# A decoder layer with routed experts: GpSimd's part of the norms and the routing, batch 3's mixing, PSUM homes, placement order and weight fills rearranged

## The chip, the cores and the metric

One core of a Trainium2 chip runs the kernel in one launch. The metric is device time in microseconds (us), the median over the runs shown. Engines are TensorE (PE; PEld its weight loads), VectorE (DVE), ScalarE (ACT), GpSimd (POOL) and SyncE (SP, which only issues DMAs here).

## What is computed

x is [4, 256, 256], the context [4, 256, 64]. Each of three sublayers is added to x:

```python
x = x + attn(layernorm(x))                 # 16 heads of 16, rotary positions, causal softmax, Wout
x = x + xattn(ctx, layernorm(x))           # per batch: (1 - g) * n + g * (A + A.T) / 2, g = sigmoid(gamma_raw), n = layernorm(x)
x = x + ffn(layernorm(x))                  # 64 experts, 6 per token, plus one shared expert
```

In xattn, sim is a 256 x 256 similarity of context rows, A keeps sigmoid(sim) where sim is among the 76 largest of its row. In ffn, the router's sigmoid scores plus a bias are looked at in 8 groups of 8; a group's score is the sum of its two largest; the 4 best groups stay, and of their experts the 6 best are taken. An expert has room for 48 tokens; the outputs are weighted by the scores (normalised, times 2.5) and summed.

## The kernel before

The 1024 tokens are 8 tiles of 128 (partitions), two tiles to a batch. The first stage does attention, mixing and routing batch by batch; then all chosen token rows lie in a DRAM table `slot_rows` (one row per expert slot), and the second stage goes over the experts in pairs: it gathers a group's slots, transposes, multiplies, and scatters the results to `expert_rows`; a tail adds them up per token and writes the output.

**The order is written by hand.** `STEPS` (L61) is one list of steps. Every engine walks it in order and executes its own part of each step; a number behind a step is the batch. The steps the text speaks of:

- A1 to A2: norm 1, projections, rotary positions, split in three bfloat16 parts. `U0` to `U5`: six score units. In step U of batch b, TensorE makes a T unit of batch b-1 and an S unit of batch b; ScalarE takes the exponentials of the T unit (L805), VectorE the row maxima of the S unit (L1168). In batch "4" only T units are left. `MS`/`MT`: the maxima split in parts (L1180 to L1183), and turned by TensorE (L513, copied at L1157). `ME`: the last PV product.
- D1a: the adjacency turned (L541) and added to itself (L1187). D1b, D1c, D1d: head outputs turned (L549), averaged (L1192, L1195), turned again (L557). D1e: output projection (`project_out`, L566), VectorE's residual (L1200) with norm 2's statistics (L1088, L1095), GpSimd's inverse root (`inverse_root`, L891 to L902).
- D2: mixing. ScalarE scales the adjacency with the norm's shift (L760), VectorE adds it to the scaled residual (L1209) and takes norm 3's statistics; GpSimd makes that root.
- D3a: ScalarE writes x3, the normed rows (L744), TensorE turns them (L574), ScalarE copies (L823). D3b: router (L584) and sigmoid (L829).
- `F n`: n steps of VectorE's adjacency work (MAX8 and MATCH_REPLACE, L1057, L1062). `R n` selects routing group n, `G n` runs n steps of VectorE's routing (L1224 to L1320; the last writes the places). `P n`: TensorE counts positions of group n (L613), between routing's selection (L1284) and the scan that is the last reader of that PSUM area (L1310). Groups 0 to 3 are the batches.
- `Z n`: GpSimd stores n slot rows (`place_rows`, L996). Each is an indirect DMA of one of a tile's six choices; 12 belong to a group, 48 in all. Those of group n wait for `place_ready` n + 1. The last group's 12 stand behind the list, behind three memsets (L1011 to L1013).

PSUM has four areas: `unit` (two halves in turn), `proj`, `gen` and `out`. `AREAS` and `USES` list from STEPS who uses an area in which order; a writer waits until the previous user has freed it.

SP's queue holds the input loads, the q/k stacks, the zeroing of the two DRAM tables, and the expert weights of pairs 0 to 21 (`later`, L359): one pair at A2d1, one at A2d2, 11 at D3a1 (which waits for the last T unit of batch 2 and all adjacency rows), 9 at D3a3. Behind them stand the waits for all placements, and the gathers.

Of the kernel before, what the change touches and what calls it, by code (L numbers as in the profile page):

```python
# [11 lines left out]
ALU = mybir.AluOpType  # L12
ACT = mybir.ActivationFunctionType
# [51 lines left out]
    D1d0 U12 A2d3 D1e0 U22 F5 U32 D20 U42 F1 D1a2 U52 F1 MS2 V0 F1 ME2 MT3 D1b1 F5 D1c1 D3a0 F6 D3b0 G9 U03 D1d1 G7 U13  # L65
    F1 D1e1 G7 U23 G4 U33 D21 U43 Z2 F1 G5 Z1 G2 P0 U53 MS3 G5 D3a1 ME3 MT4 D1b2 F4 D3b1 Z3 D1c2 R1 G1 U04 F3 G13 Z1 D1d2
    F1 Z3 U14 G2 U24 F3 D1e2 Z3 G16 U34 G5 F5 P1 U44 D22 U54 ME4 D1b3 G5 D1a3 Z1 D3a2 F1 D1c3 Z5 G5 D1d3 F2 Z4 F1 G2 D1e3
    F1 Z2 F1 D3b2 G1 R2 Z1 G48 F1 D23 Z1 P2 Z5 D3a3 F1 D3b3 Z4 F1 R3 MS4 G1
# [8 lines left out]
        "P": ("gen", "pos")}  # L77
NORMS = []
for _st, _b in STEPS:
    if _st in USES:  # L80
        AREAS[USES[_st][0]].append((USES[_st][1], _b))
# [9 lines left out]
AREAS["proj"] += [("sd", 1)]  # L91

# [4 lines left out]
def decoder_kernel(nc, x, cosT, sinT, ctxT, wxT, wqkvT, woT, gamma, gate_w, bias, w_gu, w_dn, ws_gu, ws_dn, out):  # L97
# [3 lines left out]
    with ExitStack() as ctx:  # L101
# [109 lines left out]
        gpen = cut(MO, NT, NG)  # L211
# [61 lines left out]
        var_ready, norm_ready, spread_ready = sem("var_ready"), sem("norm_ready"), sem("spread_ready")  # L273
        xn_ready, shuffled, sin_done, roped, part0, rest_ready, part1, part2 = (
# [41 lines left out]

        def probs_at(key):
            return prob[:, T_UNITS.index(key), :]
# [9 lines left out]
        def _(sp):  # L328
# [30 lines left out]
            later = {("A2d", 1): range(0, 1), ("A2d", 2): range(1, RA - 6), ("D3a", 1): range(RA - 6, RA + 5), ("D3a", 3): range(RA + 5, RP)}  # L359
            for stage, b in STEPS:  # L360
# [11 lines left out]
                if (stage, b) == ("D3a", 1):  # L372
                    filled(sp, "unit", (T_UNITS[-1], 2))
                    sp.wait_ge(adj_row, B)
                if (stage, b) == ("D3a", B - 1):
                    filled(sp, "gen", ("att", B - 1))
                for p in later.get((stage, b), ()):
                    ring_fill(p)
# [27 lines left out]
        def _(pe):  # L406
# [129 lines left out]
            def adjacency_turned(b):  # L536
                claim("gen", ("aT", b))
                pe.wait_ge(adj_row, b + 1)
                for i in range(TPB):
                    for j in range(TPB):  # L540
                        last = nc.tensor.transpose(gen[:, i * S + j * P:i * S + (j + 1) * P], adj[:, TPB * b + j, i * P:(i + 1) * P], identf[:, :])  # L541
                last.then_inc(full["gen"], 1)
# [17 lines left out]
            def project_out(b):  # L560
                claim("gen", ("att", b))
                emptied(pe, "gen", ("onT", b))
                pe.wait_ge(wo_in, 16)
                for t in range(TPB):
# [922 lines left out]
```

## Time and profile before

| what | us |
|---|---|
| median of 3 runs | 293.35 (292.18 to 296.54) |
| span of the profiled execution | 299.4 |
| busy: TensorE / VectorE / ScalarE / GpSimd | 226.2 / 207.2 / 95.6 / 134.1 |
| first slot row issued, last one issued | 133.43, 209.28 |
| first expert transpose | 217.95 |

The profile is of one execution; its span runs from its first to its last instruction, and is 6.05 us longer than the runs' median. "Idle before, releaser" names what ended an engine's idle time; "issue" and "remote" stand where no instruction of the profile explains it. The strips cut the span in 40 slices of 7.5 us.

### The profile page before, as it was taken

The numbers are of one execution on the slowest core, as the hardware profiler recorded it, in microseconds if no ns is written. First come the engines' busy times: TensorE is split into PE (matmuls) and PEld (weight loads), VectorE is DVE, ScalarE is ACT, GpSimd is POOL, SyncE is SP. The second block draws the span as 40 slices with busy tenths as digits, with TensorE's granted clock in tenths as the row PEclk, the third lists the DMA queues.
The fourth block names the chain that finished last, engine by engine and source line by source line (L and its number), as shares of the span: only waits on it lengthen the run. The fifth ranks groups of instructions, "written<-read, shape, count | busy, mean of one in ns | idle before, by whom it ended". The sixth has DMA issues, their size and how long they took to land.

```text
span 299.4 us, 5226 instructions
## 1 busy us (share of the span) xinstructions
PE 226.2 (76%) x1836; PEld 165.8 (55%) x1836; DVE 207.2 (69%) x668; ACT 95.6 (32%) x154; POOL 134.1 (45%) x182
## 2 busy tenths in 40 slices
PE   8883586598889888879566214494989999896993
PEld 3672475486678577659335103243457766653882
DVE  3699999979989998987692671912145334751697
ACT  1444530522434555566154014010013333333000
POOL 2810767616115300236677757777204655673000
PEclk9999589599999999999978755588699999999899
DMA  6608979694085999923208999990599999921996
GB/s 213 195 0 108 106 110 168 95 124 87 0 107 78 305 398 382 350 72 134 93 27 259 283 283 298 300 244 14 107 200 211 255 262 217 279 83 41 378 387 198
DMA packets 36890, 55.78 MB, mean 186 GB/s; under 512 B 6556, under 2 KB 26790, under 8 KB 36864
## 3 DMA queue, kind: packets, MB, share of 16 engines
q1 hardware_dynamic: 31680, 47.75, 62.6%
q10 hardware_dynamic: 768, 3.54, 5.7%
q0 software_dynamic: 4416, 4.15, 4.8%
q8 instruction: 15, 0.25, 0.4%
q14 instruction: 11, 0.09, 0.1%
HBM read 32.93 MB, written 25.17 MB: 194 GB/s over the span
## 4 chain that ended last, share of the span: by engine, by line
POOL 18%; PE 15%; issue 11%; DVE 10%; DMA 6%; another core or an unknown queue 4%; ACT 2%; ACTq 0%; POOLq 0%; SPq 0%; DVEq 0%
POOL slot_rows L996 15%; PE unit L644 5%; PE proj L663 3%; DMA arena<-expert_rows 2%; DVE arena L1432 2%; DMA arena<-slot_rows 2%; PE unit L630 2%; DVE arena L1168 2%; PE outp L653 1%; DVE arena L1434 1%; POOL rstd L897 1%; DVE arena L1438 1%; DMA slot_rows<-rows,arena 1%; DVE arena L1436 1%
## 5 line engine op out<-in xcount | busy, mean ns | idle before, releaser
L996 POOL DMA_INDIRECT slot_rows<-rows,arena x48 | 47.6, 992 | 23.9 <-issue 12.1
L1018 POOL DMA_INDIRECT expert_rows<-arena x28 | 28.3, 1010 | 34.0 <-ACT arena L870 27.5
L805 ACT ACTIVATE arena<-unit 128x1024 f32<-128x1024 f32 x24 | 24.6, 1024 | 42.8 <-PE unit L488 37.4
L1168 DVE TENSOR_REDUCE arena<-unit 128x4 f32<-128x1024 f32 (+1 forms) x24 | 28.9, 1212 | 3.1 <-PE unit L475 3.1
L1057 DVE MAX8 arena<-arena 128x8 f32<-128x256 f32 x80 | 30.6, 414 | 0.3
L488 PE MATMUL unit<-arena 128*128 128x256 bf16 (+1 forms) x128 | 29.2, 248 | 0.0
L1062 DVE MATCH_REPLACE8 arena<-arena 128x256 f32<-128x256 f32 x72 | 29.0, 409 | 0.0
L487 PE MATMUL unit<-arena,identb 128*128 128x128 bf16 x128 | 25.8, 222 | 0.0
L895 POOL TENSOR_SCALAR nmean<-mv 128x2 f32<-128x2 f32 x12 | 2.8, 236 | 46.0 <-DVE mv L1095 41.4
L486 PE MATMUL unit<-arena 96*128 96x128 bf16 (+1 forms) x96 | 22.3, 253 | 0.6 <-ACT arena L805 0.6
L475 PE MATMUL unit<-arena,identb 128*128 128x128 bf16 x128 | 20.8, 227 | 0.0
L855 ACT ACTIVATE arena<-unit 128x192 f32<-128x192 f32 (+1 forms) x18 | 5.6, 314 | 43.2 <-PE unit L644 27.4
L1411 DVE TENSOR_TENSOR arena<-arena,unit 128x192 f32<-128x192 f32 (+1 forms) x18 | 5.9, 330 | 19.3 <-ACT arena L855 16.7
L474 PE MATMUL unit<-arena 96*128 96x128 bf16 (+1 forms) x96 | 16.5, 257 | 3.3 <-DVE arena L1168 3.2
L456 PE MATMUL proj<-arena 128*128 128x256 f32 x64 | 16.6, 417 | 1.3 <-ACT arena L768 1.3
L870 ACT ACTIVATE arena<-proj,arena 128x256 f32<-128x256 f32 x32 | 13.6, 471 | 11.2 <-PE proj L663 6.4
L499 PE MATMUL outp<-arena 128*32 128x256 f32 x128 | 11.6, 404 | 5.5 <-ACT arena L792 4.7
L456 PEld LDWEIGHTS proj<-arena 128*128 128x128 f32 x64 | 13.3, 213 | 3.5 <-ACT arena L768 1.5
L1402 DVE COPY arena<-unit 128x384 f32<-128x384 f32 (+1 forms) x18 | 9.0, 507 | 8.4 <-PE unit L630 8.2
L487 PEld LDWEIGHTS unit<-arena,identb 128*128 128x128 bf16 x128 | 12.8, 100 | 1.2
L488 PEld LDWEIGHTS unit<-arena 128*128 128x128 bf16 x128 | 12.8, 100 | 1.1
L475 PEld LDWEIGHTS unit<-arena,identb 128*128 128x128 bf16 x128 | 13.1, 102 | 0.2
(221 smaller groups left out, 550.9 us busy)
## 6 DMA issues: line engine op xcount, KB each, us to landing
ring<-in_w_gu SPq DMA_DIRECT2D x16, 384.0 KB
expert_rows<-blank SPq DMA_DIRECT2D x8, 768.0 KB, 9.5
arena<-in_w_gu SPq DMA_DIRECT2D x16, 384.0 KB, 13.3
arena<-expert_rows SPq DMA_DIRECT2D x7, 768.0 KB, 9.2
slot_rows<-blank SPq DMA_DIRECT2D x1, 4608.0 KB, 17.3
arena<-slot_rows ACTq DMA_DIRECT2D x12, 288.0 KB
arena<-ring_dn SPq DMA_DIRECT2D x24, 128.0 KB, 4.5
ring_dn<-in_w_dn SPq DMA_DIRECT2D x16, 192.0 KB
```

The costliest lines, as they stand in the source:

```text
L456: last = mm(proj[:, m * S:(m + 1) * S], wqkv[:, c, m * P:(m + 1) * P], xnT[:, b % 2, c, :], start=(c == 0), stop=(c == 1))
L474: mm(area, qst[b % 3][0:KT, h, t * P:(t + 1) * P], kst[b % 3][0:KT, h, 0:n], start=True, stop=False)
L475: last = mm(area[:, n - P:n], identb[:, :], masks, start=False, stop=True)
L486: mm(area, kst[b % 3][0:KT, h, kt * P:(kt + 1) * P], qst[b % 3][0:KT, h, kt * P:S], start=True, stop=False)
L487: mm(area[:, 0:P], identb[:, :], masksT, start=False, stop=False)
L488: last = mm(area, sel[:, h:h + 1].broadcast_to((P, P)), nmT[:, kt * P:S], start=False, stop=True)
L805: act_fn(prob[:, n, :], unit_at((key, b)), ACT.Exp, scale=D ** -0.5).then_inc(unit_free((key, b)), 1)
L996: pool.indirect_dma_start(out=slot_dram, out_offset=bass.IndirectOffsetOnAxis(ap=place[:, t, k:k + 1], axis=0), in_=rows[:, t, :], in_offs ...
L1018: pool.indirect_dma_start(out=z_dram, out_offset=bass.IndirectOffsetOnAxis(ap=rowi[:, p:p + 1], axis=0), in_=yrow[:, p % NY, :], in_offset ...
L1057: last[i] = mark(v.max(best[:, i, :], simS[:, t + i, :] if r == 0 else work[:, i, :]))
L1062: last[i] = mark(v.match_replace(work[:, i, :], best[:, i, :], simS[:, t + i, :] if r == 0 else work[:, i, :], NEG))
L1168: v.tensor_reduce(nmax[:, t, c * u:c * u + c], unit_at((key, b)).rearrange("p (h k) -> p h k", k=n), axis=AX, op=ALU.max, negate=True).the ...
```

## The change

1. **GpSimd's roots.** For norms 2 and 3 of batches 2 and 3 (`LATE` = 2) VectorE adds eps to the variance (`variance_shifted`), GpSimd makes only the power, and VectorE the rest (`inverse_root` of VectorE).
2. **Pair sums.** For groups 0 and 1 the group score is the largest of the sums of two of its eight scores. A new step `H` on GpSimd writes the biased scores twice in a row and four sets of pair sums; VectorE takes one maximum over 32 of them in place of eleven small steps. Groups 2 and 3 keep the old way. All groups: the penalty and its addition become one instruction per tile.
3. **Batch 3.** The mixing needs no shift from ScalarE: ScalarE only scales the adjacency, VectorE scales, shifts and adds; VectorE writes x3 too. The residual goes in two halves.
4. **PSUM homes.** att of batch 3 in `proj`; the turned adjacency of batch 3 and positions 1 and 2 in `unit`; router logits of batches 2 and 3 in `out`.
5. **Order.** x3 of ScalarE has a step of its own (`N`). Of the places of F, G, Z, P and D steps many are new. Routing groups 0 and 1 have 26 steps, the others 37.
6. **Fills.** Pairs 8 to 10 are fetched at U5 of batch 2, 2 to 7 at U5 of batch 3, 11, 12 and 14 to 21 at D1b3, 13 at D1e3.

```diff
-    D1d0 U12 A2d3 D1e0 U22 F5 U32 D20 U42 F1 D1a2 U52 F1 MS2 V0 F1 ME2 MT3 D1b1 F5 D1c1 D3a0 F6 D3b0 G9 U03 D1d1 G7 U13
-    F1 D1e1 G7 U23 G4 U33 D21 U43 Z2 F1 G5 Z1 G2 P0 U53 MS3 G5 D3a1 ME3 MT4 D1b2 F4 D3b1 Z3 D1c2 R1 G1 U04 F3 G13 Z1 D1d2
-    F1 Z3 U14 G2 U24 F3 D1e2 Z3 G16 U34 G5 F5 P1 U44 D22 U54 ME4 D1b3 G5 D1a3 Z1 D3a2 F1 D1c3 Z5 G5 D1d3 F2 Z4 F1 G2 D1e3
-    F1 Z2 F1 D3b2 G1 R2 Z1 G48 F1 D23 Z1 P2 Z5 D3a3 F1 D3b3 Z4 F1 R3 MS4 G1
+    D1d0 U12 A2d3 D1e0 U22 F5 U32 D20 U42 F1 D1a2 U52 F1 MS2 V0 F1 ME2 MT3 D1b1 F5 D1c1 N0 D3a0 F6 D3b0 H0 F4 U03 D1d1 F3 U13
+    F1 D1e1 F3 U23 G6 U33 D21 U43 G8 F1 U53 MS3 P0 G12 N1 D3a1 ME3 MT4 D1b2 F4 D3b1 Z2 H1 Z1 D1c2 F2 U04 F5 D1d2 F2 U14 F2
+    U24 F3 D1e2 Z2 R1 G14 U34 D22 Z4 F2 U44 G4 F2 U54 P1 ME4 N2 G4 Z3 D1b3 D3a2 F2 D1c3 D1a3 G4 D1d3 D3b2 R2 D1e3 Z4 G4 D23 Z4 G6 N3 G15 P2
+    D3a3 G4 D3b3 G8 Z4 R3 MS4
...
+BESIDE = (("D3b", B - 2), ("D3b", B - 1))
+UNIT = (("D1a", B - 1), ("P", 1), ("P", 2))
+LATE = B - 2
...
+                if (stage, b) == ("U5", 2):
+                    filled(sp, "unit", (T_UNITS[-1], 1))
+                    fills(RA, RA + 1, RA + 2)
+                if (stage, b) == ("U5", 3):
                     filled(sp, "unit", (T_UNITS[-1], 2))
+                    fills(*range(RA - 6, RA))
+                if (stage, b) == ("D1b", 3):
+                    filled(sp, "out", (1, 3))
                     sp.wait_ge(adj_row, B)
+                    fills(RA + 3, RA + 4, *range(RA + 6, RP))
+                if (stage, b) == ("D1e", 3):
+                    filled(sp, "proj", ("att", B - 1))
+                    fills(RA + 5)
...
+                if kind != "ln1" and b >= LATE:
+                    late = n - NORMS.index(("ln2", LATE))
+                    gp.wait_ge(var_late, late + 1)
+                    gp.wait_ge({"ln2": spread_ready, "ln3": x3_ready}[kind], b)
+                    pool.tensor_tensor(rstd[:, k, :], srs[:, :], cexp[:, 0:1].broadcast_to((P, TPB)), ALU.pow).then_inc(root_ready, 1)
+                    return
...
+            def group_sums(n):
+
+                ts = slice(TPB * n, TPB * n + TPB)
+                emptied(gp, *LOGITS[n])
+                if n >= 1:
+                    gp.wait_ge(place_ready, n)
...
+                pool.tensor_tensor(twice[:, :, :, 0:8], g8, b8, ALU.add)
+                link(pool.tensor_tensor(twice[:, :, :, 8:12], g8[:, :, :, 0:4], b8[:, :, :, 0:4], ALU.add))
+                for k in range(4):
+                    end = pool.tensor_tensor(pairs[:, :, :, k, :], twice[:, :, :, 0:8], twice[:, :, :, k + 1:k + 9], ALU.add)
+                end.then_inc(group_ready, 1)
...
             place_rows(NT * KE - TPB * KE - (NT * KE - len(placements)))
-            gp.wait_ge(x3_ready, B)
-            filled(gp, "gen", ("att", B - 1))
+            gp.wait_ge(x3_last, 1)
+            filled(gp, "proj", ("att", B - 1))
...
+            def inverse_root(kind, b):
+
+                n = NORMS.index((kind, b)) - NORMS.index(("ln2", LATE))
+                k = int(kind[2]) - 1
+                ve.wait_ge(root_ready, n + 1)
...
+                if kind == "ln2":
+                    need(mark(v.tensor_scalar(rstd[:, k, :], rstd[:, k, :], gam[:, 2:3], None, ALU.mult)))
+                    mark(v.tensor_scalar(grow[:, :], rstd[:, k, :], 1.0, None, ALU.add))
+                v.scalar_tensor_tensor(shift[:, k, :], mv[:, k, :, 0], -1.0, rstd[:, k, :], ALU.mult, ALU.mult).then_inc(norm_late, 1)
+                normed(ve, kind, b)
...
+                    ends = []
+                    for t in range(TPB):
+                        r = res[:, TPB * b + t, :]
+                        ends.append(mark(v.tensor_scalar(r, r, grow[:, t:t + 1], shift[:, 1, t:t + 1], ALU.mult, ALU.add)))
+                    for t in range(TPB):
+                        r = res[:, TPB * b + t, :]
+                        ve.wait_ge(mix_scaled, t + 1)
+                        need(ends[t])
+                        end = mark(v.tensor_tensor(r, r, mix[:, t, :], ALU.add))
...
+                if n < LATE:
+                    ve.wait_ge(group_ready, n + 1)
+                    biased = twice[:, :, :, 0:8]
+                    done = mark(v.tensor_reduce(gsum[:, ts, 0:NG], pairs.rearrange("p t g k j -> p t g (k j)"), axis=AX, op=ALU.max))
+                    yield
...
+                for t in range(nt):
+                    done = mark(v.scalar_tensor_tensor(cand[:, t0 + t, 0:NE].rearrange("p (g j) -> p g j", g=NG),
+                                                       gout[:, t0 + t, 0:NG].unsqueeze(2).broadcast_to((P, NG, NE // NG)), -NEG / 10,
+                                                       biased[:, t], ALU.subtract, ALU.min))
+                    yield
```

## Rows read from the trace of the kernel before

**Rows 1.** The page: span and strips of 40 slices

```profile
span 299.4 us, 5226 instructions
...
POOL 2810767616115300236677757777204655673000
PEclk9999589599999999999978755588699999999899
DMA  6608979694085999923208999990599999921996
```

**Rows 2.** The chain of waits: start, us, what

```profile
195.23 0.97 POOL slot_rows L996
...
209.28 2.83 DMA slot_rows<-rows,arena
212.22 5.59 DMA arena<-slot_rows
217.95 0.63 PE unit L630 x4
```

**Rows 3.** GpSimd's timeline: start, us, instruction, idle before and releaser

```profile
133.43 1.24 POOL L996 DMA_INDIRECT slot_rows<-rows,arena  x1 [4.65 <-DVE arena L1320]
...
169.62 0.97 POOL L996 DMA_INDIRECT slot_rows<-rows,arena  x1 [0.30 <-issue]
170.66 0.23 POOL L895 TENSOR_SCALAR nmean<-mv 128x2 f32<-128x2 f32 x1
...
171.25 0.72 POOL L897 TENSOR_TENSOR rstd<-srs,cexp 128x2 f32<-128x2 f32 x1
...
193.72 0.99 POOL L1011 MEMSET arena<- 128x1024 f32 x1
```

**Rows 4.** Groups of instructions by form: count, busy, mean ns, idle before

```profile
L996 POOL DMA_INDIRECT slot_rows<-rows,arena x48 | 47.6, 992 | 23.9 <-issue 12.1 <-DVE arena L1320 6.9 <-POOL shift L901 2.0
...
L949 POOL TENSOR_TENSOR arena<-arena 128x1024 f32<-128x1024 f32 x3 | 7.1, 2354 | 7.7 <-DVE arena L1125 7.6
...
L901 POOL TENSOR_TENSOR shift<-nmean,rstd 128x2 f32<-128x2 f32 x12 | 2.5, 205 | 1.0
```

**Rows 5.** Timelines of VectorE, ScalarE and TensorE, 118 to 166 us

```profile
118.63 0.69 DVE L1200 TENSOR_TENSOR res<-res,gen 128x512 f32<-128x512 f32 x1 [0.22 <-PE gen L566]
...
129.56 0.42 DVE L1310 TENSOR_TENSOR_SCAN arena<-keep,arena 128x128 f32<-128x128 f32 x1
...
132.35 0.17 DVE L1320 TENSOR_SCALAR arena<-arena 128x16 int32<-128x16 f32 x1
...
144.41 0.69 DVE L1200 TENSOR_TENSOR res<-res,gen 128x512 f32<-128x512 f32 x1 [3.55 <-remote]
...
165.78 0.69 DVE L1200 TENSOR_TENSOR res<-res,gen 128x512 f32<-128x512 f32 x1 [5.17 <-issue]
...
137.17 1.03 ACT L805 ACTIVATE arena<-unit 128x1024 f32<-128x1024 f32 x1
...
151.27 1.09 ACT L760 ACTIVATE arena<-adj,shift,gam 128x256 f32<-128x256 f32 x2 [0.15 <-POOL shift L901]
153.36 1.02 ACT L805 ACTIVATE arena<-unit 128x1024 f32<-128x1024 f32 x1 [1.00 <-PE unit L488]
...
148.27 0.22 PE L613 MATMUL gen<-arena,tri 128*128 128x128 bf16 x1 [2.01 <-issue]
...
162.48 3.27 PE L566 MATMUL gen<-arena 128*128 128x256 f32 x8 [0.72 <-ACT arena L818]
```

**Rows 6.** VectorE's timeline: routing of groups 1 and 3

```profile
148.20 0.29 DVE L1289 TENSOR_TENSOR arena<-arena 128x128 f32<-128x128 f32 x1
...
150.75 0.17 DVE L1320 TENSOR_SCALAR arena<-arena 128x16 int32<-128x16 f32 x1
...
186.01 0.29 DVE L1224 TENSOR_TENSOR arena<-arena,biasb 128x128 f32<-128x128 f32 x1 [7.76 <-issue]
...
193.89 0.85 DVE L1320 TENSOR_SCALAR arena<-arena 128x16 int32<-128x16 f32 x1
```

More of the change, by code:

```diff
@@ L91 @@
 AREAS["proj"] += [("sd", 1)]
+LOGITS = [("out" if ("D3b", n) in BESIDE else "gen", ("lg", n)) for n in range(B)]
 def nth(area, name):
@@ L357, in stack, with fills @@
                             sp.dma_start(to, src).then_inc(stack_in[b], 16)
-            later = {("A2d", 1): range(0, 1), ("A2d", 2): range(1, RA - 6), ("D3a", 1): range(RA - 6, RA + 5), ("D3a", 3): range(RA + 5, RP)}
+            def fills(*pairs):
+                for p in pairs:
+                    ring_fill(p)
             for stage, b in STEPS:
@@ L536, in adjacency_turned @@
             def adjacency_turned(b):
-                claim("gen", ("aT", b))
+                area, to = ("unit", unit_at(("aT", b))) if b == B - 1 else ("gen", gen)
+                claim(area, ("aT", b))
                 pe.wait_ge(adj_row, b + 1)
@@ L583, in router @@
                         g = TPB * b + t
-                        last = mm(gen[:, t * NE:(t + 1) * NE], x3T[:, c, g * P:(g + 1) * P], gatew[:, c, :], start=(c == 0), stop=(c == 1))
-                last.then_inc(full["gen"], 1)
+                        last = mm(to[:, t * NE:(t + 1) * NE], x3T[:, c, g * P:(g + 1) * P], gatew[:, c, :], start=(c == 0), stop=(c == 1))
+                last.then_inc(full[area], 1)
             def shared_in(n):
@@ L820, in x3_dims @@
             def x3_dims(b):
-                moe_input(b)
                 filled(sc, "gen", ("x3T", b))
@@ L1240, in routing @@
                     need(lo)
[L1241 removed]
+                    done = mark(v.tensor_tensor(gsum[:, ts, 0:NG], tg(hi3), tg(lo3), ALU.add))
                     yield
[L1243 to L1248 removed]
@@ L1249, in routing @@
-                done = mark(v.tensor_tensor(gsum[:, ts, 0:NG], tg(hi3), tg(lo3), ALU.add))
-                yield
+                    biased = sbias[:, ts].rearrange("p t (g j) -> p t g j", g=NG)
                 need(done)
@@ L1309, in routing @@
                 yield
-                v.tensor_tensor_scan(fl(rank[:, ts]), fl(keep[:, 0:nt, :]), fl(kept[:, ts]), 0.0, ALU.mult, ALU.add).then_inc(free["gen"], 1)
+                v.tensor_tensor_scan(fl(rank[:, ts]), fl(keep[:, 0:nt, :]), fl(kept[:, ts]), 0.0, ALU.mult, ALU.add).then_inc(read, 1)
                 yield
```

220 lines of the change are left out of this document (152 added, 68 removed).

## The prediction

> **What bounds the kernel now.** I read the page's share rows first, then the chain of waits, then GpSimd's timeline, then VectorE's, and last ScalarE and TensorE where the first stage ends. No engine is busy throughout; but GpSimd's strip, broken by low slices elsewhere, stays at five or more in the ten slices from 135 to 210 us [rows 1]. The chain says why that stretch decides: from 195.23 to 210.25 us it is nothing but slot rows (a row is one indirect store of 128 tokens, issued by GpSimd); the last starts at 209.28, its data lands at 212.1, the gather reads take until 217.8, and the first expert transpose starts at 217.95 [rows 2]. The 89.2 us behind 210.25 are not touched by the change. So what it is worth is how far it moves the end of the 48th row.
>
> A row takes 0.99 us in the mean and follows its neighbour at 1.28 (0.97 busy, 0.31 issue) [rows 3, 4]. Forty-eight rows are 61.4 us of the 76.8 between 133.43 and 210.25. Between them lie four inverse roots of layer norms (2.2 to 3.3 us each with the gaps around them; the third one, 170.59 to 173.46, is shown in part) and three memsets (1.4 us) [rows 3]. The last twelve rows wait for two things: GpSimd must be through the other 36 and the memsets, at 195.06, and VectorE must have written the last group's places, at 194.74 [rows 3, 6]. The two feeders are 0.3 us apart. The kernel gains only if both come earlier, and loses if either comes later.
>
> **The queue order, counted.** GpSimd executes in program order, so a row listed behind a root waits for that root's input. Counted in the step list (Z steps), rows ahead of each root are: before, 10 ahead of norm 2 of batch 2, 13 ahead of norm 3 of batch 2, 23 ahead of norm 2 of batch 3, 26 ahead of norm 3 of batch 3; the timeline has the 23rd at 169.62, straight ahead of the third root [rows 3]. After: 3, 5, 12 and 16. I call the moment at which the power of norm 2, batch 3, can run **A**. Behind A there were 25 rows; now there are 36.
>
> Behind A the changed queue holds: the power, 0.75 with a gap of 0.5 behind it [rows 3]; 4 rows, 5.1; the second power with its gap, 1.25; 8 + 12 rows, 25.6; the memsets, 1.5; the last 12 rows, 11 x 1.28 + 0.97 = 15.05. Sum 49.75. Before, the first power of this pair started at 171.25 and the end came 39.0 later. The last row ends at A + 49.75, so A must be at 160.5 for no change at all. That is 5.3 us before the residual that feeds it starts in the present trace (165.78) [rows 5]. The question is therefore how early A comes.
>
> **What GpSimd sheds and takes on.** Each of the four late roots keeps only the power (0.75); the negated mean, the eps, the gamma factor, the growth and the shift (0.2 to 0.5 each [rows 4]) go to VectorE. A full root runs from 170.66 to 172.97, 2.3 us, so about 1.5 us x 2 for norm 2 and 0.9 x 2 for norm 3, 4.8 in all, is saved. The pair sums of batches 0 and 1 add six small tensor_tensor each. No such shape is in the trace: bounds are 0.2 us (the 128x2 one) and 2.35 us (128x1024) [rows 4]; 128 elements by the slope between them are about 0.47, so 2.8 us a call, 1.2 to 14 by the bounds. Batch 0's lies in GpSimd's idle time before 120 and costs nothing; if it took 14 us VectorE would wait for it at 122. Batch 1's stands between rows 2 and 3 of the new order, ahead of a point where GpSimd waits anyway.
>
> The Trainium skill speaks against moving elementwise sums there: GPSIMD Engine Reference, Engine selection, has additions on VectorE, GpSimd being about twice as slow for two inputs. VectorE does 128x128 in 0.29 us, so by that rule a sum would be about 0.6; the call is 3.5 then and the forecast does not move.
>
> **VectorE up to the first places.** Up to the residual at 118.63 nothing changes. From there the new order is: residual and statistics 1.6 [rows 5]; three adjacency steps 1.1; reduction 1.14; six routing steps (max over the pair sums, taken as 0.7: between 0.29 for 128 and 1.21 for 1024 elements [rows 4, 5]; then two MAX8, a copy, two replacements 0.9) 1.6; reduction 1.14; mixing with statistics 1.8; reduction 1.14; eight routing steps 1.9 (from the penalty to the selection); one adjacency step 0.4; sum 11.8, to 130.4. Then the last reduction 1.14 and the shift parts 0.85, to 132.4. The twelve steps that were spread before all come behind these: 2.2 us to the end of the scan and 2.7 to the places, as the same lines take from 148.20 [rows 6]. So the places of group 0 are written at 135.2 against 132.52, and the PSUM home "gen" is freed by that scan at 134.6 against 129.98 [rows 5]. The x3 transposes of batch 1 claim gen next; they followed at 131.4 and now start at 134.7. TensorE works in order: behind them stand the last PV of batch 2, MT4, D1b2, the router and the first T unit of batch 3. That unit's exponential, at 137.17 before [rows 5], comes about 3.1 later. What the edits save on VectorE (11 small routing steps of 0.17 to 0.3 per group, 2.3 us, against 0.7 for the max) is spent on ten adjacency steps brought forward, so it doesn't cover this.
>
> **From there to A.** The residual of batch 2 ran at 144.41, after a pause of 3.55 us that no instruction explains [rows 5]. If the pause does not recur, three microseconds later means 144.4 again; if it does, 147.5. Then on VectorE: residual and statistics 1.8, fourteen routing steps 3.5 (1.6 + 1.9) that now stand ahead of the root's remainder, the three small operations 0.7; ScalarE's scaling of the adjacency 1.15 [rows 5]; mixing 0.87, statistics 0.95, eps 0.2. The variance of norm 3 of batch 2 is ready at 144.4 + 9.2 = 153.6, up to 156.7. GpSimd has then placed 5 rows and stands idle, where it had placed 13. Its power with gap (1.25) and seven rows (8.95) take it to 163.8 to 166.9. That is one lower bound for A.
>
> The other is the attention of batch 3. ScalarE runs the scaling of batch 2 ahead of the exponentials of U4 and U5, so these cannot start before the mixing input is out, 151.6 to 154.7, and end two microseconds later, 153.6 to 156.7 (before: 154.38). From there to the residual the trace has 11.4 us [rows 5], and 1.8 to the variance. The new order takes 1.0 off (the transposed adjacency no longer stands ahead of the head average) and 0.5 by halves. A = 165.3 to 168.4; if TensorE keeps its upper clock (2.4 GHz) for project_out, about 1.8 instead of 3.27 us [rows 5], 163.8. The wait for positions of group 1 that held TensorE before 148.27 is gone, 2.0 us [rows 5], but it lay where ScalarE now waits for the scaling instead.
>
> Both bounds meet; I take A = 166.0, between 163.8 and 168.4. The last row ends at 215.75 against 210.25, +5.5 (ends +3.3 and +7.9).
>
> **The other feeder.** From A: the halves and mixing on VectorE leave norm 3 ready before GpSimd's power, at A + 1.25 + 5.1 + 0.75 = 173.1; x3 0.9, fifteen routing steps 3.7, positions 1.0, x3T 1.1, copy 0.6, router 1.9, sigmoid 0.3: 182.6 against 186.0. With 8.73 us of routing as before (186.01 to 194.74) [rows 6] the last places are written at 191.3, 3.4 earlier than now. GpSimd reaches the last twelve at 200.7. The change shortens the chain it aims at, and the rows that it moves behind the chain cost more. The other homes (gen, out, unit) serve this feeder, and cost nothing while it has 9 us to spare. The weight fills start at about 123 and 130 instead of 156.78, into a stretch where the DMA strip is at 3 or less; rows don't suffer, since they kept 1.28 us in the slices of full DMA load too, 165 to 202 [rows 1, 3]. I price them at 0.
>
> VectorE's new small operations may also be held by GpSimd: one L1320 took 0.85 beside the memset against 0.17 for the others [rows 6]. Eight such operations are new on the way from A to x3; 0 to 0.68 each is 0 to 5.4 us. I take 0, as for 3 of the 4 rows; the slack of 9 us covers the far end, the part ahead of A (two of them) would cost up to 1.4. The Trainium skill has this rule (SBUF — State Buffer, Who interferes with whom): VectorE and GpSimd share one pair of ports under an exclusive lock, and tensor_scalar and copies in the two-port mode are held for a whole GpSimd instruction. This trace agrees in that one row.
>
> **Forecast.** The profiled execution spans 299.4; the runs' median is 293.35, 6.05 less, and I carry that difference over. 299.4 + 5.5 - 6.05 = 298.85.
>
> **Rivals.**
> - *The rows don't bind (faster).* If the waits from 137 to 150 were the old order's own and the last exponential ends by 145, A falls at 157 and the last row ends at 206.75, 3.5 earlier: 289.85. For it: the unexplained pause of 3.55 us before the residual of batch 2, and TensorE's wait of 2.01 behind P1, which goes [rows 5]. Against it: the gen home freed 4.6 later, and the scaling behind fourteen routing steps. It decides from A = 160.5 on, one us per us. Chance 0.14; only A below 154.6 is over 2%, which can be told from no change.
> - *It washes out.* Pauses fall elsewhere, A near 160.5: 293.35. Chance 0.2.
> - *The chain is late as well.* Pause kept, half clock in project_out, held VectorE operations: A = 170.5, last row at 220.25, +10: 303.35. For it: TensorE's granted clock, in tenths, falls to 5 (1.2 of 2.4 GHz) in the three slices from 172.5 to 195, where TensorE is idle for long stretches, and project_out took 3.27 us at 162.48 [rows 1, 5]. Chance 0.16.
> - *The change doesn't do what it says*: GpSimd's pair sums cost 14 us and VectorE waits at 122: over 303, inside the last chance.
>
> **Numbers.** Forecast 0.5, own range 296 to 302. Of it a little under half lies above 299.2, where slower by over 2% begins (2% is about what a measurement of this kernel can tell from no change; the lower bound is 287.5). Slower 0.16 + 0.24 = 0.40; faster 0.08, part of the first rival, and rounded up to 0.1; same 0.50. For 8 in 10 the range runs from 288.5 to 304.
>
> **What would show it.** Right: places of group 0 at about 135; 5 rows done before the power of norm 3, batch 2, with two idle stretches of GpSimd over 3 us between 138 and 155; the residual of batch 3 at 164 to 166; the last places near 191 and the last row near 216; no idle of GpSimd from about 167 on. Wrong: the last twelve rows starting within 1 us of the last places (the feeder of VectorE binds), or A before 160.

## The result, and the profile after

The changed kernel took 304.04 us (302.7 and 305.37) against 292.86 of the kernel before beside it (292.18 to 296.54): ratio 1.0375, 95% interval 1.0257 to 1.0493. Medians here and below leave out runs over 1.5% above the fastest of their kernel in the same set, a slower state that any kernel can fall in (here 308.65 and 309.16, with which the median is the 307 of some recorded expectations). The kernel is slower. The forecast of 298.85 had the direction of the shift and was 5.2 us too low; 304.04 lies at the upper edge of the wide range (304) and above the narrow one (302). The largest single chance, 0.50, stood on no change clear of noise; slower, which came, had 0.40.

The page of the kernel after, the strips that answer to [rows 1]:

```profile
span 301.0 us, 5221 instructions
...
POOL 2811677615205312306336687787701566674000
```

In the two slices from 142.5 to 157.5 us GpSimd's strip reads 3 and 3 where it had 6 and 7, and the one from 210 us reads 7 where it had 2: work has moved from the first place to the second. GpSimd's timeline of the kernel after shows it exactly (start, us, instruction, idle before and its releaser), and answers to [rows 3]:

```profile
134.99 1.24 POOL L1077 DMA_INDIRECT slot_rows<-rows,arena  x1 [6.99 <-DVE arena L1481]
...
139.94 0.46 POOL L1057 TENSOR_TENSOR arena<-arena,biasb 128x128 f32<-128x128 f32 x1 [2.43 <-ACT arena L890]
140.36 0.32 POOL L1058 TENSOR_TENSOR arena<-arena,biasb 128x64 f32<-128x64 f32 x1
140.76 1.51 POOL L1060 TENSOR_TENSOR arena<-arena 128x128 f32<-128x128 f32 x4
...
147.47 0.72 POOL L957 TENSOR_TENSOR rstd<-srs,cexp 128x2 f32<-128x2 f32 x1 [4.05 <-DVE srs L1287]
...
154.48 0.71 POOL L957 TENSOR_TENSOR rstd<-srs,cexp 128x2 f32<-128x2 f32 x1 [3.78 <-DVE srs L1287]
...
167.26 0.71 POOL L957 TENSOR_TENSOR rstd<-srs,cexp 128x2 f32<-128x2 f32 x1 [3.06 <-DVE srs L1287]
...
173.47 0.73 POOL L957 TENSOR_TENSOR rstd<-srs,cexp 128x2 f32<-128x2 f32 x1
...
199.82 0.98 POOL L1092 MEMSET arena<- 128x1024 f32 x1
...
215.42 0.98 POOL L1077 DMA_INDIRECT slot_rows<-rows,arena  x1 [0.30 <-issue]
```

Ahead of the first three late roots GpSimd stands idle for 3 to 4 us, and from A (167.26) on it never does. The 36 rows behind A, with the two powers and the memsets, fill the time to 216.40. This is the picture that the forecast drew. Lines of VectorE, ScalarE and TensorE in the kernel after, answering to [rows 5] and [rows 6]:

```profile
133.92 0.17 DVE L1481 TENSOR_SCALAR arena<-arena 128x16 int32<-128x16 f32 x1
...
145.48 0.69 DVE L1307 TENSOR_TENSOR res<-res,gen 128x512 f32<-128x512 f32 x1 [2.54 <-PE gen L614]
...
165.07 0.42 DVE L1319 TENSOR_TENSOR res<-res,proj 128x256 f32<-128x256 f32 x1 [1.28 <-PE proj L614]
...
190.12 0.16 DVE L1481 TENSOR_SCALAR arena<-arena 128x16 int32<-128x16 f32 x1
...
141.17 1.03 ACT L866 ACTIVATE arena<-unit 128x1024 f32<-128x1024 f32 x1
...
163.87 1.97 PE L614 MATMUL proj<-arena 128*128 128x256 f32 x8
```

The residual of batch 2 has no "remote" pause in front of it here; before it had one of 3.55 us [rows 5]. The last places (190.12) are 11 us ahead of the last twelve rows (201.31). They no longer bind. The first expert transpose of the kernel after:

```profile
223.95 0.63 PE L682 MATMUL unit<-identf,arena 128*128 128x128 f32 x4 [1.29 <-DMA arena<-slot_rows]
```

| us | before | after | |
|---|---|---|---|
| end of the last slot row | 210.25 | 216.40 | +6.15 |
| from there to the first expert transpose | 7.70 | 7.55 | -0.15 |
| from there to the end of the span | 81.45 | 77.05 | -4.40 |
| span | 299.4 | 301.0 | +1.6 |
| median of the runs (293.35, 304.04), less the span | -6.05 | +3.04 | +9.09 |

So within the profiled executions the first stage lost about what was forecast (+6.15, forecast +5.5), and the second stage, which the change does not touch, was 4.4 us shorter. The last row is the riddle: the profile of before is an execution longer than its runs, that of after (302.7) the shortest of its own.

### The profile page after: what moved, and what is told of

Same layout as the page of the kernel before. It is cut to its first block, busy times and chain, and to the rows that moved or that the text cites. A ratio compares the mean times of both kernels' runs of the same rounds, so it can differ in the third digit from the quotient of the medians.

```text
span 301.0 us, 5221 instructions
## 1 busy us (share of the span) xinstructions
PE 222.9 (74%) x1836; PEld 165.5 (55%) x1836; DVE 207.6 (69%) x663; ACT 94.8 (31%) x152; POOL 134.9 (45%) x178
## 3 DMA queue, kind: packets, MB, share of 16 engines
q10 hardware_dynamic: 768, 3.54, 5.8%
## 4 chain that ended last, share of the span: by engine, by line
PE 21%; POOL 15%; DVE 12%; issue 10%; DMA 6%; ACT 2%; POOLq 0%; SPq 0%; ACTq 0%; DVEq 0%
POOL slot_rows L1077 13%; PE unit L696 7%; PE proj L715 4%; PE unit L682 2%; DMA arena<-expert_rows 2%; DVE arena L1593 2%; DMA arena<-slot_rows 2%; DVE arena L1249 2%; PE outp L705 2%; DVE arena L1595 1%; DVE arena L1599 1%; PE proj L596 1%; DMA slot_rows<-rows,arena 1%; PE outp L545 1%; POOL rstd L957 1%
## 5 line engine op out<-in xcount | busy, mean ns | idle before, releaser
L532 PE MATMUL unit<-arena 96*128 96x128 bf16 (+1 forms) x96 | 21.7, 247 | 0.6 <-ACT arena L866 0.6
L520 PE MATMUL unit<-arena 96*128 96x128 bf16 (+1 forms) x96 | 16.4, 256 | 2.8 <-DVE arena L1249 2.8
L671 PE MATMUL outp<-ones 128*128 128x384 bf16 x30 | 7.6, 432 | 13.9 <-DMA slot_rows<-rows,arena 13.9
L962 POOL TENSOR_SCALAR nmean<-mv 128x2 f32<-128x2 f32 x8 | 1.8, 227 | 35.4 <-DVE mv L1176 30.9
L671 PEld LDWEIGHTS outp<-ones 128*128 128x128 bf16 x30 | 3.7, 125 | 17.9 <-issue 17.1
L533 PEld LDWEIGHTS unit<-arena,identb 128*128 128x128 bf16 x128 | 12.6, 98 | 1.1
```

The costliest lines, as they stand in the source:

```text
L532: mm(area, kst[b % 3][0:KT, h, kt * P:(kt + 1) * P], qst[b % 3][0:KT, h, kt * P:S], start=True, stop=False)
L533: mm(area[:, 0:P], identb[:, :], masksT, start=False, stop=False)
```

## The experiments

Kernels with the same median of the kernel before in the table ran on one chip, beside it. The chips differ, so only such kernels, or ratios to the kernel before, are compared. GpSimd's queue and the second stage in each profile:

| kernel | before beside it, median | ratio, 95% interval | rows ahead of the four roots | A | end of last row | second stage |
|---|---|---|---|---|---|---|
| before | | | 10, 13, 23, 26 | 171.25 | 210.25 | 81.45 |
| before again | 301.00 | 1.0007 (0.9917 to 1.0096) | same | 170.78 | 210.24 | 81.4 |
| before, rows held back | 293.97 | 1.0282 (1.0141 to 1.0424) | 3, 5, 12, 16 | 164.11 | 217.40 | 77.15 |
| before, early fills | 301.73 | 1.0007 (0.9967 to 1.0048) | 10, 13, 23, 26 | 171.73 | 209.61 | 83.7 |
| after | 292.86 | 1.0375 (1.0257 to 1.0493) | 3, 5, 12, 16 | 167.26 | 216.40 | 77.05 |
| after again | 293.97 | 1.0424 (1.0285 to 1.0563) | same | 167.48 | 216.71 | 77.3 |
| after, old fills | 293.97 | 1.0315 (1.0184 to 1.0447) | same | 167.07 | 216.20 | 77.2 |
| after, order of before | 293.97 | 1.0172 (1.0039 to 1.0305) | 10, 13, 23, 26 | 169.99 | 211.00 | 76.9 |
| rows spread | 301.00 | 1.0324 (1.0204 to 1.0444) | 6, 11, 15, 19 | 173.04 | 218.72 | 81.8 |
| positions 0 in `unit` | 301.00 | 1.0354 (1.0261 to 1.0446) | 3, 5, 12, 16 | 169.93 | 220.86 | 82.7 |
| group 1 forward | 301.00 | 1.0497 (1.0405 to 1.0589) | 6, 11, 20, 24 | 177.77 | 223.47 | 81.5 |
| new order | 301.73 | 1.0104 (1.0062 to 1.0145) | 7, 11, 19, 25 | 168.69 | 212.24 | 83.5 |
| new order, old fills | 301.73 | 1.0011 (0.9964 to 1.0057) | 7, 11, 19, 25 | 164.13 | 211.11 | 81.3 |
| new order, mended | 299.64 | 1.0062 (1.0017 to 1.0106) | 7, 11, 20, 24 | 165.60 | 209.53 | 81.3 |

**The kernel before again**, with no edit.

> The kernel before, unchanged, for a second profile. The profiled execution on record spans 299.4 us where the runs' median is 292.9, and it holds pauses that no instruction explains (3.55 us ahead of the residual of batch 2, 3.7 and 4.1 us in the expert stage). Theory (queue order explains the 14 us): a typical execution lacks most of these pauses, spans about 291, and its last row ends at 205 to 208 instead of 210.25, so that the changed kernel's 216.4 is 8 to 11 us later and not 6. Rival (the second stage pays too): the last row ends at 210 again, the span is still 291 to 293, and the changed kernel must lose the rest behind its last row.

Measured: 300.95 us (300.65 to 303.64) where the same kernel had had 293.35. VectorE's timeline of this execution:

```profile
143.83 0.69 DVE L1200 TENSOR_TENSOR res<-res,gen 128x512 f32<-128x512 f32 x1 [3.54 <-remote]
...
165.49 0.69 DVE L1200 TENSOR_TENSOR res<-res,gen 128x512 f32<-128x512 f32 x1 [5.46 <-issue]
```

The pause of 3.55 us in front of the first residual is there again (3.54), and so is the long second stage. The profiled run took 300.65 us with a span of 298.8. The profile of before, with 299.4, therefore shows an execution of about 301, such as this chip gives, beside runs whose median was 293.35; whether it came from another chip than those runs is not on record. Neither expectation held: the last row ended at 210.24 again, as the rival had it, but the span was not 291 to 293.

**Rows held back, in the kernel before.** Nothing but GpSimd's queue is changed.

```diff
-    ... D3b1 Z3 D1c2 R1 G1 U04 F3 G13 Z1 D1d2
-    F1 Z3 U14 G2 U24 F3 D1e2 Z3 G16 ... D1c3 Z5 G5 ...
-    ... R2 Z1 G48 ...
+    ... D3b1 D1c2 R1 G1 U04 F3 G13 D1d2
+    F1 U14 G2 U24 F3 D1e2 Z2 G16 ... D1c3 Z2 G5 ...
+    ... R2 Z2 G48 ...
```

> The kernel before with nothing changed but the rows: 3, 5, 12 and 16 of them ahead of the four late roots, as in the changed kernel. Theory (queue order): the third root comes at 169 to 171 as before or up to 2 us earlier, eleven more rows stand behind it at 1.28 us, 14.1 us; the last row ends 11 to 14 us later than in the kernel before, ratio 1.036 to 1.048. Rival (rows are not what binds, the end is set by VectorE's places or by pauses): ratio 0.99 to 1.01.

Measured: 302.48 us (301.24 to 303.39) against 293.97, 8.5 more; the ratio of 1.028 is below the 1.036 that was expected, and the last row ended 7.15 us later, not 11 to 14. GpSimd's third root and VectorE's two residuals in it:

```profile
164.11 0.72 POOL L897 TENSOR_TENSOR rstd<-srs,cexp 128x2 f32<-128x2 f32 x1
...
141.42 0.69 DVE L1200 TENSOR_TENSOR res<-res,gen 128x512 f32<-128x512 f32 x1 [0.51 <-PE gen L566]
...
161.74 0.69 DVE L1200 TENSOR_TENSOR res<-res,gen 128x512 f32<-128x512 f32 x1 [5.41 <-PE gen L566]
```

Behind A stand 53.3 us against 39.0, 14.3 more: the eleven rows at 1.28 (14.1), as counted. A is 7.14 earlier, which I had not expected, and its parts can be read. The residual of batch 3 comes 4.04 earlier, 2.99 of it because the pause in front of the residual of batch 2 is missing (141.42 against 144.41 [rows 5]). And the power follows that residual by 2.37 instead of 5.47 us: in the kernel before the root waits 3.1 us behind a row [rows 3]. The other 1.05 us of the earlier residual is not traced. Net of the pause, the held-back rows put the end of the last row about 10 us later (14.3 - 3.1 - 1.05). The queue order alone, with nothing else of the change, made the kernel 2.8% slower.

**The changed kernel again**, with no edit.

> The changed kernel again, as the measure for the variants that run beside it. If the whole loss is the kernel's own, the ratio to the kernel before is 1.03 to 1.045 here too. If the first measurement was wide by chance and my queue count (+5.5 us) is right, it is 1.012 to 1.025. The last slot row should start near 215.4 us and the power of norm 2 of batch 3 (A) near 167.

Measured: 305.44 us (302.6 to 306.08), 11.5 above the kernel before, where the first measurement had 11.2; the loss is the kernel's own, and 216.71 and 167.48 are where they were expected.

**The changed kernel in the order of the kernel before.** The whole step list of before, with N0, H0, H1, N1, N2, N3 put in and eleven G steps taken from each of groups 0 and 1; for instance:

```diff
-    ... U24 F3 D1e2 Z2 R1 G14 U34 D22 Z4 F2 U44 G4 F2 U54 P1 ME4 N2 G4 Z3 D1b3 ...
+    ... U24 F3 D1e2 Z3 G16 U34 G5 F5 P1 U44 D22 U54 ME4 D1b3 G5 D1a3 Z1 N2 D3a2 ...
```

> The changed kernel with every cheaper operation and every new PSUM home kept, but with the step list of the kernel before (slot rows 10, 13, 23 and 26 ahead of the four late roots; routing of group 0 and its places where they were; x3 of each batch on its engine straight ahead of its transposes). Theory (the queue order costs the time): A falls at 164 to 169 and behind it stand 25 rows instead of 36, power and gap 1.25, 3 rows 3.8, power 1.25, 10 rows 12.8, memsets 1.5, last twelve 15.05, in all 35.7 us, so the last row ends at 200 to 205 if the last places are there by 190, and no later than 210 if they bind; the ratio to the kernel before is 0.965 to 1.00 and GpSimd has no idle stretch over 3 us between 150 and 165. Rival (the loss lies in the operations themselves, in pauses of TensorE, or behind the slot rows): the last row ends at 212 or later and the ratio stays at 1.025 or more.

Measured: 298.50 us (296.33 to 299.59). It lies between the two expectations: 6.9 us of the 11.5 come back with the order, but there is no gain on the kernel before. TensorE and GpSimd show why:

```profile
148.21 0.27 PE L665 MATMUL unit<-arena,tri 128*128 128x128 bf16 x1 [4.71 <-issue]
...
164.41 3.75 PE L614 MATMUL proj<-arena 128*128 128x256 f32 x8 [0.72 <-issue]
...
177.70 0.98 POOL L1077 DMA_INDIRECT slot_rows<-rows,arena  x1 [5.77 <-DVE arena L1481]
```

TensorE waits 4.71 us for group 1's selection (written at 148.10) ahead of the last two T units, and project_out took 3.75 us (granted clock 0.50) where it took 1.97 (1.00) in the changed kernel. A came at 169.99, straight behind the 23rd row, so the rows ahead of it held it as well. What GpSimd saves on its roots it loses waiting for group 2's places.

**The fills.** Two pairs: the changed kernel with the old fills, and the kernel before with the new ones.

```diff
-                if (stage, b) == ("U5", 2):
-                    filled(sp, "unit", (T_UNITS[-1], 1))
-                    fills(RA, RA + 1, RA + 2)
...
+                if (stage, b) == ("D3a", 1):
+                    filled(sp, "unit", (T_UNITS[-1], 2))
+                    sp.wait_ge(adj_row, B)
```

> The changed kernel with the weight fills back at their old places in SyncE's queue (all of them behind the last adjacency rows, the last four behind the attention of batch 3). Theory (fills cost nothing in either place): within 1% of the changed kernel run beside it, the last row starts within 1 us of its 215.4. Rival (the early fills disturb TensorE or VectorE through memory or DMA traffic): 1 to 3% faster than the changed kernel, fewer pauses of TensorE between 120 and 165.

> The kernel before with nothing changed but the weight fills, which go as early as in the changed kernel. Theory (early fills cost in part of the executions): ratio 1.005 to 1.012. Rival, and what my prediction priced (0): ratio 0.995 to 1.004, the last row within 0.5 us of 210.25.

Measured: 302.78 us (302.46 to 303.69) with old fills beside 305.44 with early ones, though the profiled executions of the two are as good as one (spans 300.7 and 300.8). In the kernel before early fills changed nothing (1.0007, twelve runs; the last row ended at 209.61), as the rival had it. Alone the first pair proves little, with four runs each; the next experiment has the same pair again.

**A new order**, meant to be faster than both: the old order up to group 0's places, the last T units straight behind each other, positions of group 1 behind them, fewer rows ahead of the first late root. The lines taken out are those of the changed kernel in the order of the kernel before.

```diff
-    F1 Z3 U14 G2 U24 F3 D1e2 Z3 G16 U34 G5 F5 P1 U44 D22 U54 ME4 D1b3 G5 D1a3 Z1 N2 D3a2 F1 D1c3 Z5 G5 D1d3 F2 Z4 F1 G2 D1e3
+    F1 U14 G2 U24 F3 D1e2 Z4 G9 U34 U44 U54 P1 D22 Z1 ME4 G14 N2 D1b3 D1c3 Z7 D1d3 D3a2 F11 D1e3
-    F1 Z2 F1 D3b2 G1 R2 Z1 G48 F1 D23 Z1 P2 Z5 N3 ...
+    D3b2 D1a3 R2 Z6 G48 F1 D23 Z1 P2 Z5 N3 ...
```

> The changed kernel's parts in a new order: routing of group 0 and its places as in the kernel before; the last two softmax units of batch 3 straight behind the third, the positions of group 1 behind them; norm 2 of batch 2 with 7 rows ahead instead of 10; batch 3's head average ahead of the last adjacency steps; routing of group 2 in one piece behind the residual of batch 3. Theory (GpSimd's queue and VectorE's order together set the end, so both must be right): the last exponentials end near 149 instead of 155 us, A comes at 163 to 166 with 19 rows ahead, behind it stand 29 rows, 37.1 us, two powers with gap and the memsets, 4.0 us; the last row ends at 204 to 208 against 210.25 before, 211.0 in the order of the kernel before and 216.7 in the changed kernel; ratio to the kernel before 0.975 to 0.995. Rival (the attention chain of batch 3 is held by something else, so that A stays at 168 to 170): the last row ends at 209 to 213 and the ratio is 1.00 to 1.02.

> The same order with the weight fills at their old places in SyncE's queue. With the changed kernel's own order the old places gave a median 3 us lower, though both profiled executions had the same length. Theory (early fills cost some us in part of the executions, through pauses that come and go): 2 to 3 us below the same order with early fills. Rival (chance between executions): within 1 us of it.

Measured: 305.12 us with early fills and 302.02 with old ones, twelve runs each on one chip; ratios 1.0104 and 1.0011, and their intervals do not touch. Early fills cost 0.9% in this order. The two profiles around the last T units, by stretches of 5 us (length, then busy time with number of instructions for PE, PEld, DVE, ACT and POOL, granted clock, share of the DMA engines, GB/s); with early fills:

```profile
140.00:145.00 5.00, 5.00 (x61) 4.15 (x60) 3.36 (x17) 1.65 (x2) 4.18 (x7) 1.00 1.03 362
145.00:150.00 5.00, 3.73 (x37) 2.16 (x34) 4.28 (x23) 1.94 (x2) 3.48 (x5) 1.00 1.05 354
```

and with old ones:

```profile
140.00:145.00 5.00, 5.00 (x65) 3.62 (x64) 4.77 (x20) 1.28 (x2) 3.93 (x5) 1.00 0.32 115
145.00:150.00 5.00, 2.52 (x38) 1.67 (x35) 2.87 (x19) 3.27 (x5) 3.47 (x5) 1.00 0.24 86
```

The DMA engines are full in one and a quarter to a third full in the other, and the fourth exponential of batch 3 runs at 147.48 against 143.87. Of these 3.6 us 1.45 were there at 95 us already, long before the first of the early fills; about 2.2 arise here. That the full DMA load is what delays it is suggested by this one pair of profiles and not shown, and no run shows how.

With early fills all three figures fell as the rival had them: A at 168.69, the last row's end at 212.24, the ratio at 1.0104. With old fills A came as expected (164.13, expected 163 to 166), but the last row did not (211.11). GpSimd in that kernel:

```profile
176.52 0.98 POOL L1067 DMA_INDIRECT slot_rows<-rows,arena  x1 [5.31 <-DVE arena L1471]
```

My order had group 2's router and the turned adjacency behind project_out, so that group's places were late (176.07).

**That fault mended**: the router ahead of project_out, the turned adjacency added behind group 2's routing, old fills.

```diff
-    ... N2 D1b3 D1c3 Z7 D1d3 D3a2 F11 D1e3
-    D3b2 D1a3 R2 Z6 G48 F1 D23 Z1 P2 Z5 N3 ...
+    ... N2 D1b3 D3a2 D1c3 Z8 D1d3 D3b2 F11 D1e3
+    R2 Z4 G48 D1a3 D23 Z3 P2 Z5 N3 ...
```

> The new order with old fills, with one fault mended: there GpSimd stood idle for 5.31 us until the places of group 2 at 176.07, because VectorE's routing of that group waited for TensorE to run project_out, the router and the transposes of the last adjacency in this order. Now the x3 transposes of batch 2 and the router come ahead of project_out, and the transposed adjacency is added behind the routing. Theory (with the places in time GpSimd has no idle stretch left): A at 164 to 167.5 (TensorE's router costs up to 1.3 us of it) with 20 rows ahead, places of group 2 at 171 to 174, last row ends at 204.5 to 208, ratio to the kernel before 0.975 to 0.993. Rival (TensorE's pauses and held VectorE steps take the gain, wherever the steps stand): places of group 2 at 175 or later, last row at 209 or later, ratio 0.996 to 1.01.

Measured: 301.86 us (299.18 to 303.22), ratio 1.0062, last row ended at 209.53. A (165.60) and the places of group 2 (172.75) came as expected, the end did not, for a reason of my own making:

```profile
172.75 0.17 DVE L1471 TENSOR_SCALAR arena<-arena 128x16 int32<-128x16 f32 x1
...
176.72 0.71 POOL L947 TENSOR_TENSOR rstd<-srs,cexp 128x2 f32<-128x2 f32 x1 [5.33 <-DVE srs L1277]
```

I had listed only 24 rows ahead of the fourth root, so GpSimd waited for that root with group 2's rows ready from 172.9. Three rows fitted there, 3.8 us. The rival (other pauses eat the gain) is neither shown nor refuted; no version here is faster than the kernel before.

**Three edits of the changed kernel** that loosen one link each: more rows ahead of the roots (Z4 behind H1, Z5 at D1e2, Z1 at D22, none at N2, Z3 more ahead of D1e3's root); positions 0 in `unit`, so that `gen` is free earlier; and group 1's routing and its rows brought forward.

```diff
-... D3b1 Z2 H1 Z1 D1c2 ... D1e2 Z2 R1 G14 U34 D22 Z4 F2 U44 ... N2 G4 Z3 D1b3 ... R2 D1e3 Z4
+... D3b1 Z2 H1 Z4 D1c2 ... D1e2 Z5 R1 G14 U34 D22 Z1 F2 U44 ... N2 G4 D1b3 ... R2 Z3 D1e3 Z4
```

> The changed kernel with its slot rows spread otherwise and nothing else: 4 instead of 1 behind the pair sums of batch 1, 5 instead of 2 at D1e2, 1 instead of 4 at D22, none at N2, 3 ahead of the root at D1e3; 15 instead of 12 rows ahead of the power of norm 2 of batch 3. Theory (GpSimd's idle stretches of 4.05, 3.78 and 3.06 us cost what they last): the last row ends about 3.5 us earlier, near 213, and the time falls by 3 to 4 from 307 to 303.5. More can't come back, since group 1's places are written only at 163.8 and 36 rows stand behind them. Rival (the late feeder is what costs): no change within 1 us.

```diff
-UNIT = (("D1a", B - 1), ("P", 1), ("P", 2))
+UNIT = (("D1a", B - 1), ("P", 0), ("P", 1), ("P", 2))
```

> The changed kernel with positions of group 0 in the unit home instead of gen. Theory (the x3 transposes of batch 1 waited for the scan that frees gen): they start at about 131 instead of 133.6, everything from the T units of batch 3 on comes 2.5 us earlier, the power of norm 2 of batch 3 at about 164.8 instead of 167.26, the last row at about 214 and the time 2.5 lower. Rival (VectorE's order sets the pace, the home is hidden): under 1 us.

```diff
-... U34 D22 Z4 F2 U44 G4 F2 U54 P1 ME4 N2 G4 Z3 D1b3 ... D1a3 G4 D1d3
+... U34 D22 G12 Z1 F2 U44 P1 F2 U54 ME4 N2 Z8 D1b3 ... D1a3 D1d3
```

> The changed kernel with group 1's routing brought forward: all its last 12 steps directly behind the mixing of batch 2, positions 1 in gen and ahead of U5, and the slot rows 2, 4, 5, 1, 8 so that 20 instead of 12 lie ahead of the power of norm 2 of batch 3. Theory (36 rows behind that power set the end): group 1's places are written near 157 instead of 163.8, 28 rows remain, the last row ends near 207 (216.4 less 8 x 1.28), and the time falls by 8 to 10 to about 298. Rival (batch 3's chain is what is slow): moving VectorE's work ahead of it delays the power by 2 to 3 us, and no more than 4 us come back.

None is shown to help (1.0324, 1.0354 and 1.0497; the changed kernel had 1.0375 and 1.0424 in other sets of runs). With the rows spread GpSimd does 12 rows early and then stands:

```profile
167.09 0.98 POOL L1077 DMA_INDIRECT slot_rows<-rows,arena  x1 [9.47 <-DVE arena L1481]
```

Group 1's places come at 166.65 there, so rows 13 on cannot start; the queue order is only half of it, and VectorE's order, which had pushed group 1's places from 150.75 [rows 6] to 163.62, is the other half. With group 1 brought forward (161.58) the residual of batch 2 ran only at 150.22, and A went to 177.77. That residual stands ahead of every routing step that was moved, and with the rows spread alone it ran at 145.53, so its delay is not shown to be the edit's. With positions 0 in `unit` the residual of batch 2 came 2.6 us earlier (142.88 against 145.48), but VectorE then waited 6.12 us ("remote") in front of the head average of batch 3, and A was no earlier. In all three, project_out took longer than the 1.97 us of the changed kernel: 3.73, 2.86 and 3.51 us at granted clocks of 0.50, 0.68 and 0.53, in the order of the edits. These three ran on a chip with many such pauses and without the changed kernel beside them, so small differences among them mean nothing.

## Why the prediction was right and wrong

| step of the prediction | said | measured |
|---|---|---|
| places of group 0 written | 135.2 | 134.09 |
| first exponential of batch 3 | +3.1 | +4.0 (141.17) |
| pair sums of a batch | 2.8 | 2.3 (0.46 + 0.32 + 1.51) |
| idle stretches over 3 us, 138 to 155 | two | 4.05 and 3.78 |
| residual of batch 3 | 164 to 166 | 165.07 |
| A | 166.0 | 167.26 |
| from A to the end of the last row | 49.75 | 49.14 |
| last places | 191.3 | 190.28 |
| end of the last row | 215.75 | 216.40 |

**The mechanism was right.** GpSimd's 48 rows bind, and it is the rows moved behind the root that cost most. Holding them back in the kernel before, with nothing else, gave 1.028; giving all other parts the old order brought 1.042 back to 1.017. What the remaining 1.7% are is only in part known. The rivals are out: A was not at 157 to 160.5, the loss did not wash out, the chain was not at 170.5, and the pair sums took 2.3 us, not 14.

**That A fell within 1.3 us of the forecast is in part luck.** The last exponential ended at 153.98 and TensorE ran project_out in 1.97 us at its upper clock (granted 1.00 from 163.9 to 165.8; in the kernel before 0.57 from 162.5 to 165.7): these are the conditions of the forecast's lowest case, 163.8, and A came 3.5 us later. TensorE in the kernel after, with the row of the stretch from 155 to 160 us (granted clock 0.54):

```profile
155.00:160.00 5.00, 4.20 (x43) 2.66 (x32) 1.58 (x7) 2.48 (x5) 3.89 (x5) 0.54 0.42 133
...
158.22 1.94 PE L596 MATMUL proj<-identf,arena 128*128 128x128 f32 x8 [0.80 <-ACT arena L853]
...
162.98 1.00 PE L635 MATMUL outp<-gatew,x3T 128*128 128x64 f32 x8
```

and the same two instructions in the kernel before, where the clock was 1.00 in that stretch:

```profile
157.30 1.06 PE L549 MATMUL proj<-identf,arena 128*128 128x128 f32 x8 [0.79 <-ACT arena L792]
...
166.53 1.10 PE L584 MATMUL gen<-gatew,x3T 128*128 128x64 f32 x8 [0.78 <-issue]
```

The low clock came earlier than in the kernel before and made the head transposes 0.9 us longer, and the router of batch 2, which ran behind project_out before (166.53, against 162.48), now runs ahead of it, 1.0 us that the working did not count. The rest of the 3.5 us is not traced.

**What failed is the conversion to run time**, at three places.

1. "The profiled execution spans 299.4; the runs' median is 293.35, 6.05 less, and I carry that difference over." A span cannot be longer than its own run; in every run here with both, the run is 1.7 to 1.9 us *longer* than the span. So the -6.05 was no property of the measurement. It meant that the profiled execution was some 8 us slower than the typical run, and that its rows hold something those runs lack. Carried over, it credited the changed kernel with 6.05 us; in fact its median lay 3.04 above its profiled span. This term was off by 9.09, the span by -3.9 (304.9 forecast, 301.0 measured): together the 5.2.
2. The first stage of before held a pause of 3.55 us, and the working let it drop out of the changed kernel only ("If the pause does not recur, three microseconds later means 144.4 again"). That sets a disturbed before against an undisturbed after. The kernel with held-back rows shows the old chain without it: residual of batch 2 at 141.42. Against this the changed kernel's 145.48 is 4.1 late, not 1.1. The second stage has the same fault with 4.4 us: 81.45 in the profile of before, 76.9 to 77.3 in all five profiles from the sets in which the kernel before had 293 to 294, and 81.3 to 83.7 in the other nine, that of before among them.
3. "The weight fills [...] I price them at 0." In the old order that holds (1.0007). In the new order of the experiments they cost 3.1 us, with separate intervals; in the changed kernel's own order the medians differ by 2.7, but the intervals overlap (1.0285 to 1.0563, 1.0184 to 1.0447), so there it is likely and not shown. The reason given, that rows keep 1.28 us under full DMA load, was true of GpSimd and said nothing of the other engines.

The three overlap and don't add up to one figure. The loss was 11.2 us in the first measurement and 11.5 in the second, twice the 5.5 of the forecast. The lowest run of each, 292.18 and 302.7, are 10.5 apart, which is what steps 1 and 2 leave for the first stage (5.5 + 0.65 + 3 to 3.5), within a microsecond or so.

**Open:** what the "remote" pauses are. They come at the same instructions in both profiles of the kernel before, are missing from the five profiles with the short second stage, and move when the order is changed. What the 1.7% are that stay with the old order; early fills are a candidate. Whether moving the small root operations to VectorE (part 1) or the new homes are worth anything alone was not tried.

## What to carry to other kernels

Before a profile's times are added up, compare its span with the runs' median: a span longer than the median says that the profiled execution is not a typical one, and each pause without a releaser must then be taken out of both sides of the sum, or out of neither. Where one in-order engine issues both short urgent work and a long backlog, count the backlog on either side of each urgent piece: an item moved behind it costs its full time at the end, and all that comes back is the time for which the urgent piece had been waiting behind it. Shedding work from that engine gains nothing while its backlog is held up by inputs that come late.

## What was unexpected of the hardware

- One kernel, two levels: the kernel before had medians of 292.9, 301.0, 294.0, 301.7 and 299.6 us in the five sets of runs, and the second stage of its profiles and its variants' was 77 or 81.3 to 83.7 us. The difference between these sets, up to 3%, is larger than that between most of the kernels, so only kernels run side by side can be compared. In the expert stage all nine profiles with the long second stage have a pause of ScalarE of 2.9 to 3.8 us, without a known releaser, ahead of each of the same four instructions, 6.7 to 6.8 us apart; the five with the short one have none. Two of the four in the kernel before:

```profile
246.93 0.33 ACT L855 ACTIVATE arena<-unit 128x192 f32<-128x192 f32 x1 [3.74 <-remote]
...
253.68 0.33 ACT L855 ACTIVATE arena<-unit 128x192 f32<-128x192 f32 x1 [3.68 <-remote]
```

- VectorE held by a GpSimd memset. In the changed kernel in the old order one small TENSOR_SCALAR took 1.44 us instead of 0.17 and ended at 195.39, with the memset; it began beside the row ahead of the memset (VectorE, then GpSimd):

```profile
193.95 1.44 DVE L1481 TENSOR_SCALAR arena<-arena 128x16 int32<-128x16 f32 x1
...
194.38 0.97 POOL L1092 MEMSET arena<- 128x1024 f32 x1
```

  The row of before with 0.85 [rows 6] ended with its memset too (194.74 and 194.71), and so did the same operation in the second profile of before (0.86 us) and with early fills (1.16). The Trainium skill (SBUF — State Buffer, Who interferes with whom) has VectorE and GpSimd share a pair of ports under an exclusive lock; this case agrees for the memset. A slot row can hold such an operation as well. In the new order with old fills one of 0.17 us took 0.43 and ended with the row beside it (VectorE, then GpSimd):

```profile
192.77 0.43 DVE L1471 TENSOR_SCALAR arena<-arena 128x16 int32<-128x16 f32 x1
...
192.10 1.10 POOL L1067 DMA_INDIRECT slot_rows<-rows,arena  x1 [0.30 <-issue]
```

  The same was so in this order with early fills, and for one or two small copies (0.34 to 0.46 us, each ending with its row) in each of the four profiles of the kernel before and its variants. Others beside a row kept their time, among them the new ones of the roots in the changed kernel (0.15 to 0.23), so the forecast's 0 was right for these; that rows hold none would have been wrong.
- Four additions of 128 x 128 on GpSimd took 1.51 us in a row, 0.38 each, and a single one 0.46, against 0.29 on VectorE: a factor of 1.3 to 1.6, where the Trainium skill (GPSIMD Engine Reference, Engine selection) gives about two for two inputs.
